# Cross attention with a quantised feed-forward block: GpSimd rounds the up products' input before it normalises the probabilities of the same slot

## The reference, cut to what matters

```
x = x + xattn(layernorm(x), ctx, ctx, mask)      # Q, K, V, scores, softmax, attn @ V, @ wo
x = x + ffn(layernorm(x))

def bitlinear(x, w, b):                          # used twice: up (w1) and down (w2)
    xq = act_quant(rmsnorm(x))                   # round(x * 127 / max|x|) / (127 / max|x|), by row
    return einsum('bsd,fd->bsf', xq, weight_quant(w)) + b
h   = gelu(bitlinear(x, w1, b1))
out = bitlinear(h, w2, b2)
```

## Time and profile before

| | us |
|---|---|
| median of 3 runs | 765.94 |
| the 3 runs | 765.94, 760.66, 766.47 |
| the profiled execution | 764.71 |
| its span, first to last instruction | 762.9 |

### The profile page before, as it was taken

How to read it: one execution, slowest core, us unless ns; L and a number is a source line. 1 busy time by engine, 2 the same in 40 slices (tenths; PEclk the granted TensorE clock), 3 DMA queues, 4 the chain that set the end, 5 groups by cost and what they waited for, 6 DMA issues and landing times.

```text
span 762.9 us, 13877 instructions
## 1 busy us (share of the span) xinstructions
PE 666.9 (87%) x4856; PEld 428.1 (56%) x4856; DVE 604.4 (79%) x1060; ACT 521.7 (68%) x1455; POOL 505.8 (66%) x645
## 2 busy tenths in 40 slices
PE   7756778989999999999999999999999998887885
PEld 5434566656666556556655666656655664554432
DVE  3396776789788897889887978889788778888783
ACT  2254544797578778877687767877888878777360
POOL 3056343776867777777777687767777768777664
PEclk9978889999999999999999999999999999999998
DMA  9933012043322421243334332252223233232244
GB/s 308 378 123 125 12 37 69 22 104 76 76 49 57 125 51 53 64 118 76 76 63 118 76 77 57 55 122 57 54 52 74 66 63 63 63 63 64 56 77 110
DMA packets 109204, 65.37 MB, mean 86 GB/s; under 512 B 90775, under 2 KB 90775, under 8 KB 108495
## 3 DMA queue, kind: packets, MB, share of 16 engines
q1 hardware_dynamic: 108079, 64.49, 33.8%
q10 hardware_dynamic: 1056, 0.00, 0.1%
HBM read 35.12 MB, written 8.39 MB: 57 GB/s over the span
## 4 chain that ended last, share of the span: by engine, by line
PE 36%; DVE 35%; ACT 16%; issue 5%; DMA 4%; POOL 3%; SPq 1%; ACTq 0%; DVEq 0%; POOLq 0%
PE ps_a L405 13%; PE ps_z L507 5%; DVE hid L870 5%; DVE yw L854 5%; ACT prob L693 5%; PE ps_y L522 4%; PE ps_a L435 4%; PE ps_a L478 3%; ACT hid L700 3%; DVE yq L857 2%; PE ps_t L466 2%; DVE bn L849 2%; DVE nmax L834 2%; DVE ps_s L831 2%; DVE oT_l L799 2%
## 5 line engine op out<-in xcount | busy, mean ns | idle before, releaser
L1106 POOL TENSOR_TENSOR prob<-prob,pinv 128x480 f32<-128x480 f32 x128 | 126.3, 987 | 177.5 <-DVE pinv L839 177.5
L693 ACT ACTIVATE prob<-ps_s,nmax 128x120 f32<-128x120 f32 x512 | 180.2, 385 | 34.5 <-DVE nmax L834 34.1
L507 PE MATMUL ps_z<-w1T,q_xT 128*128 128x512 bf16 x476 | 123.9, 383 | 5.6 <-DMA q_xT<-q_x 4.5
L870 DVE SCALAR_TENSOR_TENSOR hid<-ps_z,y_deq,b_row 128x512 f32<-128x512 f32 x119 | 88.6, 744 | 45.3 <-PE ps_z L507 45.3
L693 ACT ACTIVATION_READ_ACCUMULATOR prob<-ps_s,nmax 128x1 f32 x512 | 118.2, 231 | 0.0
L522 PE MATMUL ps_y<-w2T,q_hT 128*128 128x512 bf16 x480 | 114.1, 382 | 0.3 <-DMA q_hT<-xn 0.3
L831 DVE COPY_PREDICATED_SCALAR ps_s<-hidden_key,masked_c 128x480 f32 x128 | 89.5, 700 | 16.4 <-PE ps_s L456 16.4
L466 PE MATMUL ps_t<-ident,prob 128*120 128x128 f32 x512 | 79.2, 278 | 18.0 <-ACT probT L665 10.9
L834 DVE TENSOR_REDUCE nmax<-ps_s 128x4 f32<-128x480 f32 x128 | 84.1, 657 | 4.4
L665 ACT COPY probT<-ps_t 120x512 f32<-120x512 f32 x128 | 79.5, 621 | 7.6 <-PE ps_t L466 7.2
L466 PEld LDWEIGHTS ps_t<-ident,prob 128*120 128x120 f32 x512 | 59.8, 139 | 40.4 <-ACT probT L665 21.3
(11 more groups left out here) (155 smaller groups left out, 1397.6 us busy)
## 6 DMA issues: line engine op xcount, KB each, us to landing
xn<-in_x_dram SPq DMA_DIRECT2D x8, 1024.0 KB, 5.7
x<-in_x_dram SPq DMA_DIRECT2D x32, 256.0 KB, 2.7
out_dram<-x SPq DMA_DIRECT2D x32, 256.0 KB, 3.2
hid<-in_L_ffn_w_dram SPq DMA_DIRECT2D x4, 1024.0 KB, 8.8
w2T<-in_L_ffn_w_dram SPq DMA_DIRECT2D x2, 1024.0 KB, 14.0
ctx_k<-in_ctx_dram SPq DMA_DIRECT2D x8, 240.0 KB, 4.0
ctx_k<-in_mask_Bx1xSxS_ik_dram SPq DMA_DIRECT2D x7, 240.0 KB, 2.8
wk_s<-in_L_xattn_wk_dram SPq DMA_DIRECT2D x1, 1024.0 KB, 8.6
```

The lines of the kernel that those rows point to most:

```text
L507: last = nc.tensor.matmul(bank[:], q_xT[:, k % 3, i], w1T[:, i, c * CH:(c + 1) * CH], start=(i == 0), stop=(i == KD - 1))
L693: last = nc.scalar.activation(prob[:, n % 3, g * S2:(g + 1) * S2], ps_s[n % HG][:, g * S2:(g + 1) * S2], ACT.Exp, bias=nmax[:, n % 4, g:g ...
L870: v.scalar_tensor_tensor(hid[:, k % 2, c * CH:(c + 1) * CH], z_bank(FC * k + c)[:], y_deq[:, k % 8:k % 8 + 1], b1_row[:, c * CH:(c + 1) * ...
L1106: gp.tensor_tensor(pr, pr, pinv[:, n % 4].unsqueeze(2).to_broadcast([P, HG, S2]), ALU.mult).then_inc(s["prob_ready"], 1)
```

## The change

Only `slot(n)` of POOL differs: in the 29 slots that hold a `round_x(k)`, that step now stands ahead of `normalize(n - 2)`; `y_factor(k)` keeps its place. No instruction is added to the work or taken from it, and each keeps its semaphores.

```diff
             def slot(n):
+                k = tile_at(n, RX0)
+                if k is not None:
+                    round_x(k)
                 if n > 1:
                     normalize(n - 2)
                 k = tile_at(n, QH0)
@@
                     round_h(k)
                 k = tile_at(n, RX0)
                 if k is not None:
-                    round_x(k)
                     y_factor(k)
```

## The result

The changed kernel takes 782.6 us (median of 6 runs, 780.7 to 785.7) against 766.5 us (6 runs, 760.7 to 767.3): ratio 1.0225, 95% interval 1.0187 to 1.0262. It is 2.2% slower, some 16 to 17 us, where 10.7 had been forecast. The profiled execution took 780.73 us, its span is 778.9 us, and PE's mean granted clock fell from 0.97 to 0.95.

A forecast was written before the change was run, and what follows sets the result against it. The loop was taken to be held by ACT and POOL, with some room on PE. Terms 7.0 + 0.6 + 0 + 1.5 + 1.6 = 10.7 us on 764.7 gave 775.4 us; forecast spread 768 to 783, whole range 762 to 787.

The forecast's parts named there:

- (e): On PE, longer gaps ahead of L466 at 16 places lower the granted clock, one or two more dips: 1.6 us.
- (a): DVE's L854 ahead of tiles 2, 6, 18 and 22 starts inside POOL's L1120 and turns slow: 7.0 us.
- Arrival times: On POOL, round_x and q_x come 1.06 us earlier, the normalisation 1.38 us later, y_factor starts where it did.
- The earlier q_x is worth nothing: SP's queue, not POOL, held the q_xT transpose PE waits for: 0 taken, 5.1 us at most.
- (b): At tiles 1, 5, 9, 13, 17, 21 the late key projection slightly delays ACT's square: about 0.1 us each, 0.6.
- D: PE's delay where L466 directly follows the normalisation: 1.10 us, or 1.47 us at tiles whose L854 was quick.
- the room: Spare time between the key projection's end on PE and ACT taking it: 1.06 us.
- (c): At tiles 2, 6, 10, 14, 18, 22 idle time of DVE and L854 absorbs the delay: 0.
- (d): Tiles 25 to 28 have less around them; each loses between 0 and D, 0.4 taken: 1.5 us.
- the clock falls at half of the 16 places: On PE, new gaps beside existing idle time bring seven more clock dips: 786 us, chance 0.13.
- The rival of the mask step: The moved normalisation on POOL blocks DVE's L831, making the exponentials late: 14.5 us, so 779, chance 0.03.

The follow-up runs named there:

- the 13 slots with room: New order only in the slots with n mod 16 = 8 or 12 and tile 0, against the kernel before: 766.26 us, ratio 1.0024.
- PE alone: Kernel before, POOL's order unchanged, with twelve identity transposes ahead of L466 in the six slots with n mod 16 = 0: 771.46 us, ratio 1.0064.
- the first experiment: Four kernels, each with the new order in one group of slots only, against the kernel before: 766.26, 779.58, 768.17 and 763.50 us.
- the four slots alone: New order only in the four slots of the last sequence, against the kernel before: 763.50 us, ratio 0.9983.
- the halves: Kernel before with POOL's L1120 issued as two instructions of 128 x 1024: 750.82 us, ratio 0.9812.

## Why the prediction was right, and where its sizes were off

The direction, the places and the path were as forecast. 782.6 us is at the upper edge of the 768 to 783 given to the forecast itself, some 5 us above the sum. In the profile (e) was 6.4 us too small and (a) 1.8 too large, so the two errors cancel in part.

- *Arrival times.* Right. The normalisation came 1.30 us later by the starts (forecast 1.38), because from L1075's start to the next normalisation's it takes 312.25 - 310.88 = 1.37 us, where 1.47 had been taken from another successor. PE's L466 went with it at 16 places, 27.0 us in all (forecast 26).
- *The earlier q_x is worth nothing.* Right in effect: the 13 slots with room show no gain. PE's waits for q_xT in the slots (tile 13 and three more) are gone from the changed kernel's trace, where the prediction had expected the same count. That gave nothing: at tile 13 the first product starts 8.28 us after L863's start, before 8.33.
- *(a) The race, 7.0 us.* The mechanism is shown with PE alone (ratio 1.0064, about 5 us) and at tiles 6, 18 and 22 with 1.75 us each. Tile 2 was counted wrongly: L854 starts 0.29 us ahead of L1120 there and stayed ahead. In the profile (a) is 5.2 us. Tile 10 was slow by chance in the profile before; it is quick (0.49 us) in those of the three kernels of the first experiment that leave the slot of tile 9 as it was. Against such an execution the change loses tile 10 too, and the forecast's four races come out right by luck: tile 2 wrongly in, tile 10 wrongly out.
- *(b) Key projection, 0.6.* D and the room were both about 1.1 us, as said: with PE kept busy, tile 6's period in the changed kernel is 20.17 us, against 20.16 at tile 10 of the kernel before, where the race was lost and PE was not late. So D itself costs 0.01 us there, not 0.1. What (b) missed is its consequence: with no room left, the slow clock behind those slots goes into the loop, 1.3 to 1.6 us each time.
- *(c) n mod 16 = 4, 0.* Right within the whole change: the periods of tiles 7, 11, 15, 19 and 23 are 19.68 to 19.70, before 19.66 to 19.68.
- *(d) The last sequence, 1.5.* 1.6 in the two profiles, but the four slots alone gave a ratio of 0.9983. It is not a loss that can be told from none.
- *(e) PE's clock, 1.6.* This is the term that was mis-sized. In the profile it is 9.5 - 1.5 = 8.0 us, of which 6.7 stand behind slots with n mod 16 = 0; keeping PE busy gives 9 us back. One or two dips more were assumed; between 140 and 600 us there are 6 instead of 1, and in the last sequence 3 instead of 2, one of them twice as long. The forecast had put seven more dips into the rival "the clock falls at half of the 16 places" with a chance of 0.13 and a time of 786. That rival came true in good part, on top of the forecast's case: behind tiles 1, 9, 17 and 21, all n mod 16 = 0. At tile 9 PE idles 1.26 us ahead of L412 and 1.17 us more ahead of L466, with 0.66 us of work between: two gaps nearly in a row. The same two stand at tiles 17 and 21, and at tile 1 there is one of 2.26 us. But tile 5 has the same two gaps and the clock stayed at full speed behind it, and at tile 13, with one gap of 1.18 us, it stayed up too. So such a slot makes a fall likely, not certain. The gap of 1.26 us ahead of L412 was visible at tiles 5, 9, 17 and 21 in the trace of before, and the new gap should have been added to it slot by slot.
- *The rival of the mask step.* It did not happen: L831 takes 0.71 us beside the moved normalisation, and the exponentials keep their place. By the Trainium skill, "SBUF — State Buffer", section "SBUF: two separate sides", a DVE instruction with two SBUF inputs contends for one exclusively held port pair with a GpSimd instruction that reads SBUF. The two-input L854 agrees with that (2.25 us behind L1120, 0.69 alone), and one of its inputs is a single column spread over the row. L831 also reads two operands from SBUF, the mask and a single column, writes to PSUM, and does not wait. What sets the two apart no run here shows; the prediction was right to go by L831's own row.

Not settled: why the 13 slots with room give a ratio just above 1 (1.0024), why the clock falls behind some of the slots with equal gaps and not behind others, which part of the 9 us lies in the last sequence, and how the 20 us between the two kernels with a two-input L854 divide.

## What to carry to other kernels

Before a step is moved ahead of another on a helper engine, look who picks up the one that is passed and how soon: 0.15 us of distance at 16 places, not the engine's idle time, decided here. Where one engine's instruction has to wait for the whole of another's, as L854 for L1120, the length of the longer one is a price for the other; cutting GpSimd's 1.90 us rounding into four took 2.6% off this kernel, and whether L854 starts 0.06 us ahead of it or behind is worth 1.75 us. A new gap on PE is to be added to the gaps beside it, because the clock that falls behind them can cost as much as the wait (1.3 to 1.6 us here, behind a wait of 1.17).

## What was not expected of the hardware

- A DVE instruction slips in between two back-to-back GpSimd instructions: L854 went between the halves (1.15 us instead of 2.0) and delayed the second half by 0.17 us.
- The two-input tensor_tensor waits for GpSimd like the one-input tensor_scalar (2.25 and 2.0 us beside an L1120 that started 0.2 us earlier).
- Ten transposes of the identity (1.25 us) in the gaps of 16 slots kept the granted clock up at all but two stretches and gave back about 9 us of 783.
- Tiles 9 and 5 have the same two gaps of PE, 1.26 and 1.17 us, and the granted clock fell to 0.50 behind the first and stayed at 1.00 behind the second.
